# A three-layer field-interaction kernel: pair order, split work, PSUM banks and TensorE's order changed

## What is computed

```
X0 = inputs.reshape(-1, 32, 64)
for W, b in ((W1, b1), (W2, b2), (W3, b3)):
    Wr = W.reshape(out_ch, 32, m)
    Xi = einsum('bhd,bmd,ohm->bod', X0, Xi, Wr) + b[None, :, None]
    pools.append(Xi.sum(axis=-1))
return concatenate(pools, -1) @ fc_W.T + fc_b
```

## Time and profile before

| what | value |
|---|---|
| median of 3 runs | 99.2 us (98.79 to 99.52) |
| profiled execution, whole | 99.33 us |
| its span in the trace | 97.1 us |
| TensorE (PE) busy | 73.2 us |
| VectorE (DVE) busy | 55.4 us |
| GpSimd (POOL) busy | 40.1 us |
| ScalarE (ACT) busy | 32.8 us |

### The profile page before, as it was taken

How to read it: one execution, slowest core, us unless ns; L and a number is a source line. 1 busy time by engine, 2 the same in 40 slices (tenths; PEclk the granted TensorE clock), 3 DMA queues, 4 the chain that set the end, 5 groups by cost and what they waited for, 6 DMA issues and landing times.

```text
span 97.1 us, 992 instructions
## 1 busy us (share of the span) xinstructions
PE 73.2 (75%) x325; PEld 51.4 (53%) x325; DVE 55.4 (57%) x49; ACT 32.8 (34%) x48; POOL 40.1 (41%) x39
## 2 busy tenths in 40 slices
PE   0080995989980599964099199999999999999941
PEld 0040482845310277643065176888888888887810
DVE  0148914995900005679979999999993020332472
ACT  5409404284391221370480583463460200000000
POOL 5624049719027000069976065009029705523500
PEclk9999999999999555999957958999999999999998
DMA  2999999999999999924000960820000000000000
GB/s 71 294 255 323 389 353 378 390 225 192 266 272 226 399 331 362 215 60 123 15 0 0 283 256 10 310 115 0 0 7 0 0 0 0 0 0 0 0 0 0
DMA packets 7686, 14.86 MB, mean 153 GB/s; under 512 B 771, under 2 KB 4099, under 8 KB 7043
## 3 DMA queue, kind: packets, MB, share of 16 engines
q1 hardware_dynamic: 7251, 14.03, 46.2%
q10 hardware_dynamic: 432, 0.79, 4.0%
HBM read 12.98 MB, written 1.05 MB: 144 GB/s over the span
## 4 chain that ended last, share of the span: by engine, by line
PE 52%; DMA 21%; issue 8%; DVE 5%; ACT 4%; SPq 4%; POOL 4%; DVEq 0%; ACTq 0%
DMA zz<-z_lo 13%; DMA x<-x 8%; PE x_ps L521 8%; PE a_ps L521 8%; PE a_ps L524 8%; PE a_ps L529 8%; PE x_ps L529 7%; PE x_ps L524 6%; POOL feat L253 2%; ACT feat L312 2%; PE x_ps L541 2%; PE a_ps L560 2%; PE a_ps L559 2%; SPq L174 2%; PE z_ps L513 1%
## 5 line engine op out<-in xcount | busy, mean ns | idle before, releaser
L521 PE MATMUL x_ps<-feat,w_hi 128*128 128x512 f32 x32 | 13.7, 518 | 8.0 <-issue 4.9
L253 POOL TENSOR_TENSOR feat<-z_b,feat 128x1024 fp32r<-128x1024 f32 x4 | 9.7, 2426 | 18.4 <-ACT feat L312 18.4
L253 POOL TENSOR_TENSOR feat<-r_in,feat 128x1024 fp32r<-128x1024 f32 x4 | 10.0, 2499 | 15.0 <-ACT feat L312 15.0
L408 DVE TENSOR_TENSOR xs<-x_in,xs 32x512 fp32r<-32x512 f32 x8 | 10.1, 1266 | 9.4 <-ACT xs L312 9.3
L529 PE MATMUL x_ps<-feat,w_hi 128*128 128x512 f32 x32 | 12.5, 477 | 3.1 <-POOL feat L253 2.2
L312 ACT ACTIVATE feat<-z_ps 128x1024 fp32r<-128x1024 f32 x8 | 8.2, 1024 | 18.6 <-DVE z_ps L427 17.3
L449 DVE SCALAR_TENSOR_TENSOR x<-a_ps,vec,x 128x512 f32<-128x512 f32 x8 | 6.0, 749 | 14.2 <-PE a_ps L560 14.2
L521 PEld LDWEIGHTS x_ps<-feat,w_hi 128*128 128x128 f32 x32 | 7.3, 247 | 11.5 <-issue 5.3
L427 DVE TENSOR_TENSOR z_ps<-x_in,z_ps 128x1024 f32<-128x1024 f32 x4 | 4.9, 1229 | 12.4 <-PE z_ps L513 12.4
L524 PE MATMUL x_ps<-feat,w_lo 128*128 128x512 f32 x32 | 12.0, 460 | 0.0
L260 POOL TENSOR_TENSOR x<-x 128x512 f32<-128x512 f32 x6 | 7.8, 1292 | 9.1 <-DVE x L449 9.0
(11 more groups left out here) (67 smaller groups left out, 90.6 us busy)
## 6 DMA issues: line engine op xcount, KB each, us to landing
w_sb<-w SPq DMA_DIRECT2D x8, 512.0 KB, 9.3
r_in<-xr SPq DMA_DIRECT2D x4, 1024.0 KB, 6.6
x_in<-xl SPq DMA_DIRECT2D x8, 256.0 KB, 6.6
w_sb<-w SPq DMA_DIRECT2D x1, 768.0 KB, 5.0
a_by_fields<-at_sb SPq DMA_DIRECT2D x2, 384.0 KB, 5.4
x<-x SPq DMA_DIRECT2D x2, 256.0 KB, 7.8
zz<-z_hi ACTq DMA_DIRECT2D x2, 256.0 KB, 9.8
x<-x SPq DMA_DIRECT2D x1, 512.0 KB, 14.5
```

The lines of the kernel that those rows point to most:

```text
L253: nc.gpsimd.tensor_tensor(feat[:, c, 1, of_half(1), :], z_of(c, 1), feat[:, c, 0, of_half(1), :].bitcast(f32), ALU.subtract).then_inc(lo_d ...
L408: nc.vector.tensor_tensor(xs[rows, c, :], x_in[rows, c % X_BUFS, :], xs[rows, c, :].bitcast(f32), ALU.subtract).then_inc(xs_lo, 1)
L521: nc.tensor.matmul(bank, high[:, k, :], feat[:, c, 0, k, :], start=(k == 0), stop=False)
```

## The change

Six parts, all in one version. (1) PICKED is 6: TensorE gathers the right fields of six chunks, two r_in loads of 1 MB are left, and x_in has four buffers. (2) The low part of x is made by GpSimd for chunks 1 to 7; the sum of w1 goes from GpSimd to VectorE in return. (3) The PSUM banks of the two halves change places from chunk to chunk (field_bank), so half 0 of a chunk takes the banks that half 1 of the one before left after its multiplication; half 1's products go to a part of r_in in SBUF. (4) The data for zz (x16) are loaded before w1, and all three spread16 are issued early on ScalarE. (5) TensorE's order is written out in pieces: picks of later chunks stand between the terms of x1, and the four rounds of A stand apart, two and two. (6) ScalarE saves two rounds at once and SyncE stores A in two halves of three DMAs each. The fields of tile k on partition group j are at shift 4j+k in place of 4k+j, which makes the load of the transposed triangle (f2) one contiguous run for each field.

```diff
-PICKED = 4
-X_BUFS = 3
+PICKED = 6
+X_BUFS = 4
...
+        def field_bank(c, half):
+            return z_ps[:, (c + half) % 2, :, :]
...
-            return z_b[:, c % 2, :, :] if c < PICKED else r_in[:, c % 2, of_half(1), :]
+            if c < PICKED:
+                return r_in[:, 1, of_half(c % 2), :]
+            return r_in[:, c % 2, of_half(1), :]
...
-            def store_a(rows, g, left):
-                sp.dma_start(bass.AP(scratch.tensor, left * M, [[EXT * M, rows], [1, HALF * M]]),
-                             at_sb[64 * g:64 * g + rows, :, :].rearrange("r t n -> r (t n)")).then_inc(a_out, 16)
+            def store_a(rows, g, i, left):
+                sp.dma_start(bass.AP(scratch.tensor, (left + HALF // 2 * i) * M, [[EXT * M, rows], [1, HALF // 2 * M]]),
+                             at_sb[64 * g:64 * g + rows, 2 * i:2 * i + 2, :].rearrange("r t n -> r (t n)")
+                             ).then_inc(a_out, 16)
...
-            sp.wait_ge(a_saved, ROUNDS)
-            store_a(EXT, 0, 0)
-            store_a(EXT, 1, HALF)
-            store_a(H, 0, H)
-            load_right(PICKED + 1)
-            load_x(5)
+            for i in range(2):
+                sp.wait_ge(a_saved, i + 1)
+                store_a(EXT, 0, i, 0)
+                store_a(EXT, 1, i, HALF)
+                store_a(H, 0, i, H)
+            load_x(6)
...
-                    scratch.tensor, (J * k + j) * M, [[(EXT + 1) * M, H], [J * M, TILES - k], [1, M]])).then_inc(f_main_in, 16)
+                    scratch.tensor, (TILES * j + k) * M, [[(EXT + 1) * M, H], [1, (TILES - k) * M]])).then_inc(f_main_in, 16)
...
+            for c in range(4):
+                pool.wait_ge(xs_lo, min(c + 3, PICKED))
+                lo(c)
+                if c + 3 < PICKED:
+                    pool.wait_ge(lo_done[1], c + 1)
+                    split_x(c + 3)
...
+            def a_round(t):
+                pe.wait_ge(w2_in[t], 16)
...
+                if t == 2:
+                    pe.wait_ge(a_saved, 1)
```

More of the change, by code:

```diff
@@ L415, in mult @@
                     dve.wait_ge(picked, count(c, half))
-                    right = z_ps[:, tiles, :]
+                    right = field_bank(c, half)
                     if half == 1 and c >= 2:
@@ L479, in _ @@
             rest_lo(f1, a_hi, a_lo_done)
-            split_x(6)
             mult(6, 1)
@@ L504, in pick_right @@
             def pick_right(c, half):
-                if half == 0:
-                    pe.wait_ge(xs_lo, c + 1)
+                pe.wait_ge(xs_lo, c + 1)
                 if c >= 1 and half == 0:
+                    pe.wait_ge(z_done, count(c - 1, 1))
+                if c >= 1 and half == 1:
                     pe.wait_ge(lo_done[0], c)
-                if c >= 1 and half == 1:
-                    pe.wait_ge(z_done, count(c - 1, 1))
-                for k in range(half * PER_HALF, (half + 1) * PER_HALF):
-                    last = nc.tensor.matmul(z_ps[:, k, :], pick[:, k, :], xs[:, c, :], start=True, stop=True)
@@ L514, in pick_right @@
-                last.then_inc(picked, 1)
-            def main_terms(bank, c, half, high, low, high_done, low_done, between=None):
-                pe.wait_ge(hi_done, count(c, half))
-                pe.wait_ge(*high_done)
-                tiles = range(half * PER_HALF, (half + 1) * PER_HALF)
-                for k in tiles:
-                    nc.tensor.matmul(bank, high[:, k, :], feat[:, c, 0, k, :], start=(k == 0), stop=False)
-                pe.wait_ge(*low_done)
-                for k in tiles:
-                    nc.tensor.matmul(bank, low[:, k, :], feat[:, c, 0, k, :], start=False, stop=False)
-                if between is not None:
-                    pick_right(between, half)
-                pe.wait_ge(lo_done[half], c + 1)
-                for k in tiles:
-                    nc.tensor.matmul(bank, high[:, k, :], feat[:, c, 1, k, :], start=False, stop=False)
@@ L531, in x1_half, with terms @@
-            def x1_half(c, half):
+                for k in range(PER_HALF):
+                    last = nc.tensor.matmul(field_bank(c, half)[:, k, :], pick[:, half * PER_HALF + k, :], xs[:, c, :],
+                                            start=True, stop=True)
+                last.then_inc(picked, 1)
+            def terms(bank, c, half, weights, part, start=False):
+                for k in range(half * PER_HALF, (half + 1) * PER_HALF):
+                    nc.tensor.matmul(bank, weights[:, k, :], feat[:, c, part, k, :],
+                                     start=(start and k == 0), stop=False)
@@ L532, in x1_half, with x1_hi @@
+            def x1_hi(c, half):
                 if c >= 2 and half == 0:
                     pe.wait_ge(x1_saved, c - 1)
-                main_terms(x1_ps[c % 2][:, :], c, half, w1_hi, w1_lo, (w_hi_done, 1), (w_lo_done, 1),
-                           c + 1 if c + 1 < PICKED else None)
+                pe.wait_ge(w_hi_done, 1)
+                pe.wait_ge(hi_done, count(c, half))
+                terms(x1_ps[c % 2][:, :], c, half, w1_hi, 0, start=(half == 0))
+                pe.wait_ge(w_lo_done, 1)
+                terms(x1_ps[c % 2][:, :], c, half, w1_lo, 0)
@@ L537, in x1_tail, with x1_lo @@
+            def x1_lo(c, half):
+                pe.wait_ge(lo_done[half], c + 1)
+                terms(x1_ps[c % 2][:, :], c, half, w1_hi, 1)
             def x1_tail(c):
@@ L554, in a_product @@
                     pe.wait_ge(q_saved, 1)
+                pe.wait_ge(a_hi_done, 1)
                 for half in range(HALVES):
-                    main_terms(bank, c, half, a_hi, a_lo, (a_hi_done, 1), (a_lo_done, 1))
+                    pe.wait_ge(hi_done, count(c, half))
+                    pe.wait_ge(lo_done[half], c + 1)
+                    terms(bank, c, half, a_hi, 0, start=(half == 0))
+                    terms(bank, c, half, a_hi, 1)
+                pe.wait_ge(a_lo_done, 1)
+                for half in range(HALVES):
+                    terms(bank, c, half, a_lo, 0)
                 pe.wait_ge(xs_lo, c + 1)
```

269 lines of the change are left out of this document (150 added, 119 removed).

## The result

The changed kernel takes 91.7 us (median of 4 runs, 90.95 to 92.78) beside 99.0 us (97.92 to 99.52); the ratio is 0.927, 95% interval 0.920 to 0.934. The forecast was 92.3 us with a range of 88.3 to 96.0. Some executions of each of these kernels come out over 1.5% longer than its fastest one; the ratios leave them out, the medians don't, and the profiled execution of the changed kernel is one of them. It took 92.78 us with a span of 90.7, where the other three have spans of 88.8 to 89.8 us and no profile. So its stages are read here, and not its total against another's.

A forecast was written before the change was run, and what follows sets the result against it. Before the first A product, VectorE's order after a late start bounds the kernel; afterwards A's round trip through HBM. First A product at 53.6, plus 36.45 gives a 90.05 span, plus 2.23 makes 92.3 us; range 88.3 to 96.

The forecast's parts named there:

- a fixed stretch: From the start of the first product with A to the end of the span, TensorE at full rate: 36.45 us.
- The first A product: Start of TensorE's first product with A, forecast at 53.6 us where it was 60.65.
- The last part of w2: Landing of the weights that round 3 of A waits for: 29.5 us, range 27.6 to 31.
- round 3's end: End of the last of A's four rounds on TensorE, 0.95 us a round: 30.5 us.
- Stores: From the end of A's save to A in HBM: 6.3 us, taken between 5.4 and 7.1.
- Loads: A's loads back from HBM, 3.65 us of issue and 3.5 to landing: 7.15 us.
- From F to the first A product: From the landing of A's loads (F, 45.1 us) through the sum and chunk 5: 8.5 us, handovers included.
- the second rival: GpSimd becomes the bound, its low part of chunk 4 holding up A's sum by the port (+1.2): 95.1 us, chance 0.14.
- Zz: Its copies issued from about 10.4 us, all there between 24.4 and 29, taken as 27.
- the slower rival: Zz's copies served strictly in turn, zz there at 42.3 and the first tail holding up A's rounds: 106.0 us, chance 0.04.
- Picks: Two more chunks picked on TensorE, 0.9 us a chunk; VectorE then multiplies from PSUM, 1.23 us mean instead of 1.92.

The follow-up runs named there:

- experiment 6: The kernel before, with VectorE's main sum of A moved ahead of chunk 5: 99.5 us, ratio to the kernel before 1.008.
- experiment 4: The changed kernel without the three copies that build zz (zz filled with zeros, 16 pairs left out of the result): 89.71 us.
- experiment 7: The changed kernel with GpSimd's low part of chunk 4 ahead of xsum, and xsum started after VectorE's main sum of A: 91.54 us, ratio 0.910.
- Experiment 3: The changed kernel with A stored whole by three DMAs after the second save, as before the change: 92.65 us, ratio 0.936.
- experiment 12: The changed kernel, both port waits taken out, zz copies issued after all of w3 and the tails needing zz behind all four rounds of A: 92.48 us.
- experiment 9: The changed kernel with four chunks picked; right fields of chunks 4 and 5 loaded, one load ahead of A's loads: 95.26 us, ratio 0.969.
- Experiments 9 and 11: 11: the changed kernel with experiment 9's edit, picks of chunks 3 to 5 later, and low parts of x back on VectorE: 96.39 us, ratio 0.978.
- Experiments 5 and 6: 5: the kernel before, with zz's data loaded ahead of w1, its product first on GpSimd and its three copies issued early: 100.25 us, ratio 1.004.

## Why the prediction was right

The account of the kernel before holds in its main line: the end is the first A product plus a fixed stretch (36.45 forecast, 36.44 measured), and A had slack before (experiment 6). The account of what comes after holds too: A's round trip is the chain, and VectorE waits for it. The first A product was forecast at 53.6 and came at 54.26 in the profiled execution, and at about 52.3 to 53.4 in the others by the estimate above. That is nearer than the terms deserve: several were off, they cancelled, and this part of the agreement is luck:

- *The last part of w2*, put at 29.5 and round 3's end at 30.5: it set nothing, and the forecast sign of it, a wait that ends at 29 to 30, didn't come. TensorE's only wait in the second pair of rounds was 0.32 us for the save. What was late was V, since the last part of w3 landed at 21.4, where experiment 4 made V without a wait by 19.6. After the wait of 2.00 us for w3 the granted clock was 0.56 until 24.0 (the lower of the two levels), which I hadn't counted either. The rounds ended at 32.7, 2.2 us later than forecast. In experiment 7, the same kernel up to here, the wait for w3 was 0.81 us, the clock stayed at 1.00, a part of w2 was the last to come, and the rounds ended at 31.4 (from the chain that ended last):

```profile
11.91 15.25 DMA w_sb<-w
...
27.20 1.10 PE a_ps L608 x4
```

  I had counted the early zz only as 0.25 MB of competing bytes; the runs show a rate cut to half.
- *Stores*, 6.3 us forecast: 4.0 measured, under my lower bound of 5.4. Experiment 3 gives 6.7 without the halves, near the 7.1 of before, so it is the halves that I had valued too low. The other kernels with halves took 3.6 to 5.2 us where the trace shows the landing, and 6.8 in experiment 12, where the zz copies were under way. A was in HBM at 37.7 (37.9 forecast).
- *Loads*, 7.15 forecast: 5.1 (37.71 to 42.77), since the last one landed 1.86 us after its issue and not 3.5; and my sum counted its 0.43 us of issue twice. The row that I had taken is from a stretch with a load of 1 MB just ahead. The contiguous runs of f2 have no part in it that shows: in experiment 6, with the old pair order, f1's and f2's loads both landed after 2.2 us.
- *From F to the first A product*, 8.5 forecast: 11.5 measured (42.77 to 54.26). Of the missing 3.0, 2.1 are the sum and 1.2 the low part of chunk 5, each behind the other engine's instruction. This was the second rival's mechanism. It had named the first place, at 1.2 us, and not the second. Its sign came too: GpSimd's low part of chunk 4 released TensorE in x1_product(4), after 1.37 us. Its reason did not: GpSimd's new operation and xsum (2.64 us) were short, and it was only that the instructions stood side by side.
- *Zz*: its last copy was issued at 12.50 and took 12.5 us, so it was there at 25.0 (27 forecast); the slower rival never came near.
- *Picks*: costed by VectorE's durations. Experiments 9 and 11 show that most of their worth lies in SyncE's queue, as one load less ahead of A's. I had costed the removed loads only as VectorE's inputs, and said that 1.75 MB stand ahead of the stores as before, without asking what the load of chunk 5 had done ahead of A's loads.

The Trainium skill's rule on the port pair (page SBUF — State Buffer, section SBUF: two separate sides: an exclusive lock for a whole instruction, where the later one blocks) agrees with the trace here in both directions: 2.80 us for VectorE's sum at 42.77 behind GpSimd's operation, and 3.59 for GpSimd's at 49.67 behind VectorE's.

What stays open is which part freed the kernel before. Each part that I took back alone cost 0.5 to 1.5 us by the medians (0.9 to 1.8 by the ratios), but for the picks with their load (3.6, of which the traces show 2.3), and three together cost 4.7 of the 7.3 us. The rest should lie in what stayed: early zz with the fourth buffer and the load order, the exchange of banks, the halves, the parted rounds, the place of the sum and ScalarE's order. Experiments 5 and 6 show only that early zz and the place of the sum do nothing alone on the kernel before, the first since it then delays x's chunk 3. The fourth buffer, the load order and the parted rounds weren't tried by themselves.

## What to carry to other kernels

When the bound moves from one chain to another, most parts taken back alone will look small, because the new bound covers them; read for each what stands in the wait that now ends last, and cost a removed DMA by the queue that it stood in, not only by who used its data. Where two engines can lock each other out, write down which instruction of the other engine stands beside each step of the chain: one reordered line and two waits were worth another 2 us here. And a chain that sums to the right total may do so by cancelling errors; check it stage by stage.

## What the runs showed of the hardware

- Three copies from SBUF to SBUF of 256 KB each, into 32 partitions at a time, went with a DMA rate of half for some 7 us, their own bytes included (183 to 187 GB/s against 388 to 414 with the copies left out), while the DMA engines' busy share stayed at 1.06 to 1.08. The kernel before has 184 GB/s from 20 to 24, and the slow time moves with the copies (experiment 12). Whether the 32 partitions or the crossing of two queues is the cause wasn't tried.
- GpSimd's subtraction on 32 partitions by 512 elements takes 1.27 us, and on 128 by 512 also 1.27: between these two the number of partitions made no difference.
- The issue of a DMA on SyncE took 0.30 to 0.45 us in most places and over 0.9 in others (3 stores in 2.81 us before; of the last three of the changed kernel, two show 0.30 and 0.42). Full DMA engines alone aren't the reason: a load of x at 16.70 in the changed kernel took 0.33 us with their share at 1.07 to 1.10.
- A load of 64 KB of A landed 1.9 us after its issue in the changed kernel, and after 4.3 to 4.5 behind a load of 1 MB in the same queue (experiment 9).
